# The lower bound of a clip moved from SBUF to a PSUM bank, and the edges' products in two banks instead of three

## The reference, cut to what matters

```python
def layer0(x, edge_row, edge_col, edge_val, W):
    agg = segment_sum(edge_val[:, None] * x[edge_col], edge_row)
    return relu(einsum('ni,oi->no', agg, W))

def layer1(x, src, dst, ...):
    npj = relu(layer_norm(x @ Wp + bp, gp, betap))                      # 20 values a node
    kron = einsum('ea,ek->eak', npj[src], npj[dst]).reshape(E, -1)      # 400 values an edge
    kron = relu(layer_norm(kron @ Wk + bk, gk, betak))                  # 256 values an edge
    kron_feat = segment_sum(kron, dst)
    logits = relu(concatenate([x[dst], x[src]], 1) @ We + be)
    a = softmax of logits over the edges of each dst
    context = relu(segment_sum((x @ Wn + bn)[src] * a, dst))
    ...                                       # GRU cell, layer norm, last linear layer
x = layernorm(x + layer0(...)); x = layernorm(x + layer1(...))
```

## Time and profile before

| | |
|---|---|
| median of three runs | 8942.02 us (8932.08 to 8956.04) |
| the profiled execution | 8936.67 us, span of its records 8935.2 us |
| PE busy | 6445.6 us, 72% of the span |
| DVE busy | 5818.1 us, 65% |
| POOL busy | 4539.2 us, 51% |
| ACT busy | 3738.4 us, 42% |
| the clip, L1635 | 2608 instructions, 1088.3 us |
| the copy out of PSUM, L1575 | 1962 instructions, 815.0 us |

### The profile page before, as it was taken

The page is one execution under the profiler, slowest core; times in us unless marked ns, Lnnn a source line. Parts: engine busy times, 40 slices in busy tenths (PEclk is TensorE's granted clock), DMA queues, the critical chain, the costliest instruction groups (busy, mean ns, idle before and its releaser), DMA issues.

```text
span 8935.2 us, 169603 instructions
## 1 busy us (share of the span) xinstructions
PE 6445.6 (72%) x32727; PEld 4098.9 (46%) x32728; DVE 5818.1 (65%) x16429; ACT 3738.4 (42%) x10876; POOL 4539.2 (51%) x4743
## 2 busy tenths in 40 slices
PE   3244666666666699987767777777777777777888
PEld 2221444444444477763334444444444444444444
DVE  8896444444444466665547778777777777776666
ACT  0000444444444300003336666666666666665433
POOL 0000777777778500000017777777777777775100
PEclk9676777877787799996669999999999999999998
DMA  0002333333322388865557877777877888776200
GB/s 13 0 0 75 94 99 100 99 99 99 100 97 95 118 263 262 263 229 226 223 221 213 214 213 215 214 214 212 215 214 213 214 215 215 211 216 182 59 19 18
DMA packets 973553, 1399.03 MB, mean 157 GB/s; under 512 B 378858, under 2 KB 744924, under 8 KB 960328
## 3 DMA queue, kind: packets, MB, share of 16 engines
q1 hardware_dynamic: 761663, 797.51, 29.6%
q0 software_dynamic: 208448, 596.38, 23.6%
q10 hardware_dynamic: 3012, 1.51, 0.1%
HBM read 986.32 MB, written 415.51 MB: 157 GB/s over the span
## 4 chain that ended last, share of the span: by engine, by line
PE 31%; issue 18%; DVE 18%; DMA 12%; SPq 8%; ACT 7%; POOL 4%; DVEq 2%; ACTq 1%; POOLq 0%
DMA arena_n<-rec_dram 8%; SPq L550 7%; PE ps L1991 6%; PE ps L1889 5%; PE ps L1786 4%; PE ps L2009 3%; ACT junk L993 3%; POOL msg_dram L814 3%; PE ps L2000 3%; DMA arena_e<-msg_dram 2%; DVE arena_e L1635 2%; PE ps L1904 2%; DVE arena_r L1297 2%; DVE arena_e L1575 2%; ACT L1014 1%
## 5 line engine op out<-in xcount | busy, mean ns | idle before, releaser
L835 POOL DMA_INDIRECT arena_n<-tab_dram,idxs x2624 | 2744.4, 1046 | 2374.1 <-DVE idxs L1550 1575.3
L1991 PE MATMUL ps<-arena_n 126*128 126x257 f32 x5234 | 1677.5, 417 | 582.7 <-DVE arena_e L1575 562.7
L814 POOL DMA_INDIRECT msg_dram<-arena_e,idxq x1616 | 1634.8, 1012 | 434.3 <-issue 425.2
L1991 PEld LDWEIGHTS ps<-arena_n 126*128 126x128 f32 x5234 | 841.8, 193 | 1144.8 <-DVE arena_e L1575 1005.3
L1878 PE MATMUL ps<-arena_n,arena_r 128*128 x3232 | 1096.1, 498 | 354.8 <-ACT arena_r L902 354.8
L1575 DVE COPY arena_e<-ps 128x257 f32<-128x257 f32 x1962 | 815.0, 421 | 528.3 <-ACT junk L993 514.6
L1635 DVE SCALAR_TENSOR_TENSOR arena_e<-arena_e,rstd,nbetak_b 128x256 f32<-128x256 f32 x2608 | 1088.3, 480 | 31.6 <-DVE rstd L1641 31.1
L993 ACT ACTIVATE junk<-ps 128x256 f32<-128x256 f32 x2617 | 985.3, 382 | 203.5 <-PE ps L1991 188.6
L1878 PEld LDWEIGHTS ps<-arena_n,arena_r 128*128 128x128 f32 x3232 | 758.7, 246 | 595.7 <-issue 466.9
L907 ACT ACTIVATE arena_e<-ps,recq 128x256 f32<-128x256 f32 x1616 | 739.3, 475 | 662.6 <-PE ps L1878 653.9
L1889 PE MATMUL ps<-arena_e,oh 128*128 128x256 f32 x3520 | 816.7, 387 | 88.3 <-DVE oh L1351 86.8
(11 more groups left out here) (333 smaller groups left out, 9126.7 us busy)
## 6 DMA issues: line engine op xcount, KB each, us to landing
arena_n<-m_dram SPq DMA_DIRECT2D x2624, 126.5 KB
arena_e<-msg_dram SPq DMA_DIRECT2D x441, 514.0 KB, 4.4
m_dram<-arena_e SPq DMA_DIRECT2D x49, 1413.5 KB, 4.9
m_dram<-arena_e SPq DMA_DIRECT2D x49, 1285.0 KB, 4.5
arena_n<-tab_dram,idxs POOLq DMA_INDIRECT x2624
hist_dram<-arena_r SPq DMA_DIRECT2D x163, 253.0 KB
arena_n<-rec_dram SPq DMA_DIRECT2D x1616, 2.0 KB
msg_dram<-arena_e,idxq POOLq DMA_INDIRECT x1616
```

What stands on the lines that cost most here:

```text
L814: nc.gpsimd.indirect_dma_start(out=msg_dram, in_=msgs[:, u, j, :], in_offset=None, out_offset=bass.IndirectOffsetOnAxis(ap=idxq[:, u, j:j ...
L835: nc.gpsimd.indirect_dma_start(out=feat[:, u, i, :], out_offset=None, in_=tab_dram, in_offset=bass.IndirectOffsetOnAxis(ap=idxs[:, u, i:i ...
L1991: mm(ps[:, bank_of(i), 0:HC], prods_t[0:KM, s % 2, j * P:(j + 1) * P], m_ring[0:KM, i, :], start=True, stop=True).then_inc(e_h, 1)
```

## The change

The clip's bound is copied once into bank 3 of PSUM, ahead of the edge stage, and each clip reads it there in place of the SBUF tile `nbetak_b`. Bank 3 is taken from `linear`: tile i now goes to bank 1 + i % 2, and waits for the copy of tile i - 2. The order of the instructions on each engine stays the same.

```diff
         def bank_of(i):
-            return 2 if i == SG - 1 else 1 + i % 3
+            return 1 + i % 2
 
         def last_in_bank(i):
 
-            return {0: 4, 1: 2, 2: 4, SG - 1: 2}.get(i, 3)
+            return 2
...
             step(nc.vector.memset(acc[:, :, :], 0.0))
+            floor = ps[:, 3, 0:D]
+            step(nc.vector.tensor_copy(floor, nbetak_b[:, :]))
...
                     h = hgb[:, u % 2, i, 1:HC]
-                    stt(out=h, in0=h, scalar=rstd[:, u % 2, i:i + 1], in1=nbetak_b[:, :],
+                    stt(out=h, in0=h, scalar=rstd[:, u % 2, i:i + 1], in1=floor,
                         op0=ALU.mult, op1=ALU.max).then_inc(e_clip, 1)
```

## The result

The changed kernel takes 9849.4 us (median of 4 runs, 9834.6 to 9854.4) against 8945.0 us: 1.1009 times as long, interval 1.099 to 1.1028. That is 904 us more; 9730 was predicted, within 9550 to 9910.

What follows compares the result with a forecast made beforehand. No engine is full in the edge stage; written order and waits between engines set the time. Terms 745 - 18 + 65 + 0 = 792 us on 8936.7 gave 9729, predicted as 9730 us (8.8% slower), range 9550 to 9910.

Steps and rivals of the forecast that it cites:

- The ring: Edge stage: waits that ran side by side now form one chain, 25.33 us a group against 20.76, 745 us in all.
- from A to A: One step's length, between starts on PE of linear j=1 in successive steps; forecast 7.01, 6.24, 5.47 and 6.61 us.
- s0 to s3: The four steps of one edge-stage group, forecast together at 25.33 us against 20.76 before.
- C - B: Time between starts of DVE's copies of j=1 and j=2, taken as unchanged: 1.98, 1.90, 1.13 and 0.93 us.
- The costly link: PE's linear j=0 of the next step must wait for DVE's copy of j=2, with the softmax products queued behind it.
- L = C + 0.48: PE's linear j=0 of the next step starts 0.48 us after DVE's copy of j=2 starts.
- The links called hidden: Linear j=2 waiting for the copy of j=0, and j=3 for that of j=1, were to add no time.
- ScalarE's way: ACT's square and copy of j=3 ahead of the next linear j=1: 1.60 us, deciding in the second and third steps.
- The operand: Clip with its bound in PSUM: 473 ns against 480, off the chain, so 0 us in the sum.
- The loop's end: Where the loop branches back, ACT's late evacuation overlaps added waits, giving back 0.46 x 40 = 18 us.
- The clock: TensorE's clock falls in one in six of 2 x 163 PE stretches in s0 and s1, 1.2 us each: 65 us.
- The rival of a fall in each s0 and s1: TensorE's clock falls in both steps of every group: 489 us in place of 65, 10153 us; chance 0.10.

Runs made afterwards that it cites:

- wait_j0: Kernel before with three banks, but linear j=0 of the next step also waits for the copy of j=2; 11576 us, 1.0314 times the kernel before.
- changed_again: The changed kernel as it stands, run again beside the kernel before in a later set, where the loop stalled; 11772 us, 1.0356 times the kernel before.
- banks_alone_again: The changed kernel with two banks but the clip's bound read from SBUF; 11716 us, 1.0312 times the kernel before.
- short_turns_in_s0: Kernel before with three banks, its two early returns of a bank moved from tiles 15 and 1 to 3 and 5; 11234 us, 0.9888 times it.

## Why the prediction was right

- *The ring.* Predicted 7.01, 6.24, 5.47 and 6.61 us from A to A for s0 to s3, measured in the group at full clock 6.80 (6503.78 to 6510.58), 6.45, 5.40 and 6.70 (to 6529.13, PE's next row of that kind). Together 25.35 against 25.33. The single terms are off by up to 0.2 us and cancel, and that is luck. In s0 PE's turn and sums took 1.64 us (6508.94 to 6510.58) where I had read 1.87; no wait is shown within them in either trace, and why they are faster is open. In s1 C - B is 2.18 us in place of 1.90, as it is in one of the four groups of the loop, before as after; I had read the rows of another group. Over the whole stage groups at full clock take 25.1 to 25.35, some 25.2 in the mean: 4.45 x 162 = 721 us of the 904, against 745.
- *The costly link.* L = C + 0.48 was the step on which all hung. `wait_j0` and the brackets of L1993 show it. The links called hidden cost nothing beside it: with all four waits s0, s1 and s3 are no longer than with j=0 alone. ScalarE's way decides in s2 by 0.26 us, predicted 0.35. PE's two waits in s0 came as estimated, 1.16 and 1.28 us against 1.2 and 1.3.
- *The operand.* 477 ns against 473 taken and 480 before; off the path, as said: two banks alone have the same steps. The mean record of a gather (L835 on GpSimd) is 969 ns with the bound in PSUM and 993 with it in SBUF (`changed_again`, `banks_alone_again`); what that is worth, if anything, no run shows. Of the rule that an operand from PSUM costs a higher fixed term (the Trainium skill, "VectorE: DVE Perf Modes", "The TRN2 errata"), this pair of operands shows nothing: 3 ns less, not 65 more.
- *The loop's end.* Groups with it take 29.13 us in the mean, 3.9 over the ring, against 24.88 - 20.75 = 4.13 before. Given back 0.2 x 39 = 8 us, predicted 18.
- *The clock.* This is the term that was mis-sized, threefold. I took a fall in one of six long stretches at 1.2 us, 65 us in all. There were 183 stretches at the lower level against 32, about one a group, most of them in s0, at 1.6 us (6.5 against 4.9 from C to B). Groups without the loop's end take 26.78 in the mean, 1.58 over the ring: 1.58 x 123 = 194 us. The three terms, 721 - 8 + 194 = 907, make up the 904. Two thirds of the s0 are at the lower level, not one in six; the mean group of 26.8 us is close to the 27 from which I had called the forecast wrong. The rival of a fall in each s0 and s1 at 489 us was too much; away from the loop's end fewer than one s1 in five takes over 4.6 us.
- The Trainium skill, "TensorE: Matmul & The Clock Gate", section "A second HAM failure mode: psum-queue depth-cycling", describes a clock that swings when PE pauses between groups while it cycles through banks; this trace agrees, with the mean granted clock of the stage at 0.91 in place of 0.98, and shows no more than the coincidence.
- *The signs.* PE's wait for the copies is 2.2 times what it was, not several times; the mean clock of 0.91 is a little over the bound of 0.9; the group with the loop's end takes 29.1 us, 28.4 predicted.

## What to carry to other kernels

With a fixed order on each engine, the number of buffers decides which waits run side by side. Before taking one away, write down for each producer which consumer it will wait for and what stands in both queues between the two: here one wait moved from B to C put PE's sums and DVE's products, that had overlapped, one behind the other, at 4.5 us a group, while the operation the buffer was given to gained 3 ns. If slots don't divide the work evenly, the place of the early return is free to choose; moving it gained 1% here, with 0.41 us of each group seen in the step that it left.

## What was not expected of the hardware

The same two waits of PE (1.16 and 1.28 us, a linear between) left TensorE's clock at the lower level in about two of three groups and at the full one in the rest (111 and 51 of 162), and a fall cost 1.6 us of 25. And the loop that ran at 20.75 us a group in the first profiles stalled 4 to 7 us about twice a group in all later runs, in every kernel, behind a releaser that the profile doesn't name; with it the loss of the change shrank from 10.1% to 3.6%. A part of that is s0, which takes the same time with two banks and three when it is stalled (C to B most often 8.6 us in `banks_alone_again` and in `short_turns_in_s0`).
